# One fused recurrent block on one core: new due times for the planned order, the experts' first block among them

## The reference

```python
xn = layernorm(x)
x  = x + attention16heads(xn) * silu(moe(xn))            # 160 experts, top 8, plus a shared one
xn = layernorm(x)
x  = x + mamba2layers(xn) * silu(coupling_net_3cycles(xn))

def moe(x):
    probs = sigmoid(x @ router_w.T + bias)
    w, idx = top_k(probs, 8); w = 2.5 * w / (sum(w) + 1e-9)
    return sum_k w_k * (silu(x @ gate[idx_k].T) @ down[idx_k].T) + shared(x)

def mamba(x, p):                       # state of 16, 256 inner channels, scan along the sequence
    u = silu(conv4(x @ in_w)); delta = softplus(...)
    h[t] = exp(delta * A) * h[t-1] + delta * B[t] * u[t];  y[t] = C[t] . h[t]
    return (y + D * u) * silu(z) @ out_w
```

## Time and profile before

| | before |
|---|---|
| median of 3 runs | 2323.13 us (2319.16 to 2328.2) |
| profiled execution | 2325.84 us, span 2324.0 us, mean granted clock 0.887 |
| PE busy | 1946.7 us (84%) |
| DVE busy | 1648.5 us (71%) |
| POOL busy | 1500.2 us (65%) |
| ACT busy | 1312.4 us (56%) |
| DMA | 321.50 MB, mean 138 GB/s |

### The profile page before, as it was taken

One profiled execution on the slowest core, in us unless ns is written; L12 is line 12 of the kernel. 1 busy time (PEld: TensorE's weight loads), 2 busy tenths in 40 slices (PEclk: granted clock), 3 DMA queues, 4 the chain that ended last, 5 costly groups with the idle time before them and its releaser, 6 DMA issues. The chain is left out here.

```text
span 2324.0 us, 29708 instructions
## 1 busy us (share of the span) xinstructions
PE 1946.7 (84%) x8440; PEld 878.5 (38%) x8440; DVE 1648.5 (71%) x3485; ACT 1312.4 (56%) x2685; POOL 1500.2 (65%) x1476
## 2 busy tenths in 40 slices
PE   4576499999998898986787787899898898899976
PEld 2343266665655555553333332222222222222221
DVE  3877165665656756667466414999999899999998
ACT  3354154554534445354577656777766666667663
POOL 0388485774355745407653002999999999999997
PEclk9779799999999999998788888898888898888896
DMA  9931387786665756641110004555555555555552
GB/s 379 395 86 59 89 243 216 227 237 190 202 191 150 221 147 174 188 120 51 42 35 24 1 3 106 116 120 115 114 114 119 124 125 129 130 129 128 129 125 43
DMA packets 210968, 321.50 MB, mean 138 GB/s; under 512 B 28914, under 2 KB 102644, under 8 KB 210420
## 3 DMA queue, kind: packets, MB, share of 16 engines
q1 hardware_dynamic: 194420, 286.02, 45.2%
q0 software_dynamic: 16384, 33.59, 5.1%
HBM read 207.29 MB, written 112.20 MB: 137 GB/s over the span
## 5 line engine op out<-in xcount | busy, mean ns | idle before, releaser
L1498 DVE TENSOR_TENSOR_SCAN db<-pa,db 128x512 f32<-128x512 f32 x512 | 597.5, 1209 | 46.1 <-POOL db L1549 29.7
L1549 POOL TENSOR_TENSOR db<-dur,bb 128x1024 f32<-128x1024 f32 x256 | 596.9, 2356 | 48.5 <-DMA bb<-bc_scratch 39.7
L1479 ACT ACTIVATE pa<-dlr,an 128x510 f32<-128x510 f32 x512 | 340.2, 681 | 188.2 <-DVE db L1498 187.3
L1022 POOL DMA_INDIRECT yg<-y_disp,idx x256 | 257.6, 1006 | 185.6 <-DMA y_disp<-yb 85.7
L725 POOL DMA_INDIRECT x_disp<-xt,idx x256 | 254.4, 994 | 149.2 <-DVE p L699 93.4
L860 ACT ACTIVATE pr<-sm,nbi 128x128 f32<-128x128 f32 (+1 forms) x512 | 228.1, 447 | 209.4 <-DVE nbi L883 204.6
L907 POOL TENSOR_SCALAR pr<-pr,rcp 128x128 f32<-128x128 f32 x320 | 134.9, 432 | 244.7 <-DVE rcp L892 242.3
L1404 PE MATMUL pb<-db,rw_all 128*32 128x512 f32 x1024 | 209.9, 698 | 79.3 <-DVE db L1504 47.8
L883 DVE CUSTOM_DVE_ANT_0 sm<-pa,rw_front 128x128 f32<-128x128 f32 (+1 forms) x512 | 161.1, 352 | 105.2 <-PE pa L780 104.7
L143 ACT ACT_TABLE_LOAD x146 | 187.3, 1283 | 56.3 <-DVE lg L587 16.3
L790 PE MATMUL pb<-rw_all,pr 128*128 128x128 f32 x768 | 143.3, 298 | 73.7 <-DVE ptt L877 49.6
(11 more groups left out here) (292 smaller groups left out, 3387.7 us busy)
## 6 DMA issues: line engine op xcount, KB each, us to landing
wb<-in_wexp SPq DMA_DIRECT2D x576, 96.0 KB
x_disp<-yb SPq DMA_DIRECT2D x8, 4608.0 KB, 30.1
xb<-x_disp SPq DMA_DIRECT2D x144, 256.0 KB
y_disp<-yb SPq DMA_DIRECT2D x144, 256.0 KB
dlr<-d_scratch SPq DMA_DIRECT2D x128, 256.0 KB, 5.3
dur<-d_scratch SPq DMA_DIRECT2D x128, 256.0 KB, 8.3
bb<-bc_scratch SPq DMA_DIRECT2D x64, 256.0 KB
d_scratch<-dl SPq DMA_DIRECT2D x32, 256.0 KB, 5.8
```

What stands on the lines that cost most here:

```text
L1022: e.e.indirect_dma_start(out=YG[:, t % 2, j, :], out_offset=None, in_=YD[h], in_offset=bass.IndirectOffsetOnAxis(ap=IDX[:, c:c + 1], axis= ...
L1479: e.e.activation(decay(a).rearrange("p (b l) -> p b l", b=2)[:, :, 1:256], DLR[:, h % 2, i % 4, :].rearrange("p (b l) -> p b l", b=2)[:, : ...
L1498: e.e.tensor_tensor_scan(hk(a), decay(a), hk(a), 0.0, ALU.mult, ALU.add).then_inc(s_scan, 1)
L1549: e.e.tensor_tensor(DB[:, b % ND, :, :], DUR[:, h % 2, 2 * (b % 2):2 * (b % 2) + 2, :], BB[:, b // 2 % 4, :].rearrange("p (o l) -> p o l", ...
```

## The change

Only numbers of `PL` change: no instruction is added or taken away, no tile, no semaphore. So every engine has the same instructions in another order. The quads' first due time goes from 1.3234 to 1.4811 and their step from 2.6979 / 72 to 2.605 / 72; some sixty other offsets move a little.

```diff
--- before.py
+++ after.py
@@ -41,87 +41,87 @@
 
 
 PL = {'net_a': 0.3,
- 'quad0': 1.3234,
- 'quads': [2.6979, 2.6979],
+ 'quad0': 1.4811,
+ 'quads': [2.605, 2.605],
  'after0': 22,
  'after': 14,
  'back': [7.0971, 7.4103, 7.7, 8.32],
- 'pick0': 3.5729,
- 'picks': 3.5546,
+ 'pick0': 3.5611,
+ 'picks': 3.532,
  'pick1': 6.8429,
  'picks1': 0.2953,
  'net': [7.2386, 8.4094],
  'nets': [0.06, 0.0472],
  'qload': 1.9826,
- 'qcopy': 0.31,
- 'qgate': 0.8265,
- 'qtanh': 1.2037,
- 'qstt': 1.2651,
- 'qdown': 1.7277,
- 'qyb': 2.0102,
+ 'qcopy': 0.3818,
+ 'qgate': 0.7876,
+ 'qtanh': 1.1564,
+ 'qstt': 1.301,
+ 'qdown': 1.708,
+ 'qyb': 2.0168,
  'qout': 2.8324,
  'sum': 10.1825,
- 'b_sg': 0.2077,
+ 'b_sg': 0.1951,
  'b_sth': 0.3731,
- 'b_hs': 0.4677,
- 'b_cb': 0.5793,
+ 'b_hs': 0.4663,
+ 'b_cb': 0.4909,
  'b_th': 0.5906,
  'b_gs': 0.7618,
- 'b_m': 0.7165,
+ 'b_m': 0.7504,
  'b_c': 0.9108,
- 'b_sq': 0.7871,
- 'b_v': 0.7661,
- 'b_ln': 0.91,
+ 'b_sq': 0.833,
+ 'b_v': 0.8202,
+ 'b_ln': 0.9574,
  'b_x': 0.5141,
  'u_ex': 0.8912,
- 'u_pt': -0.8853,
+ 'u_pt': -0.8732,
  'u_sm': 0.4089,
  'u_pn': 0.2408,
- 'u_k': -2.1136,
- 'u_kc': -1.6411,
- 'norm0': 0.0219,
- 'norm': 0.0142,
+ 'u_k': -2.2911,
+ 'u_kc': -1.621,
+ 'norm0': 0.0238,
+ 'norm': 0.0111,
  'normu': 0.0118,
  'routeA': [0.0993, 0.0297],
- 'routeB': [0.547, 0.0536],
- 'placeA': [0.35, 0.016],
- 'placeB': [0.9637, 0.0164],
+ 'routeB': [0.5312, 0.0536],
+ 'placeA': [0.361, 0.016],
+ 'placeB': [0.9872, 0.0151],
  'unit0': 0.4143,
  'PG': [0, 1, 1, 1, 1, 1, 0, 0],
- 'sends': 73,
- 'l_m': 0.0097,
+ 'sends': 74,
+ 'l_m': 0.0136,
  'l_xi': [0.1133, 0.1982],
- 'l_z': [0.1831, 0.2458],
- 'l_bc': 0.349,
+ 'l_z': [0.1831, 0.2705],
+ 'l_bc': 0.3492,
  'l_dt': [0.3955, 0.3884],
  'l_ds': [0.6084, 0.716],
  'l_out': 0.4456,
  'l_c': -2.4568,
  'l_y': [4.4386, 6.8066],
- 'l_sq': -0.0665,
- 'l_ln': 0.0497,
- 'l_u': [0.1938, 0.3298],
- 'l_bf': 0.411,
- 'l_ab': [0.4595, 0.4956],
+ 'l_sq': -0.0481,
+ 'l_ln': 0.0464,
+ 'l_u': [0.187, 0.3298],
+ 'l_bf': 0.379,
+ 'l_ab': [0.4595, 0.4733],
  'l_ex': 0.5125,
- 'l_w': 0.5414,
- 'l_v': 0.49,
- 'l_lp': 0.5743,
- 'l_dl': [0.6663, 0.7761],
- 'l_da': -2.8788,
+ 'l_w': 0.5459,
+ 'l_v': 0.5264,
+ 'l_lp': 0.5653,
+ 'l_dl': [0.6663, 0.7804],
+ 'l_da': -2.8649,
  'l_hn': 0.0022,
- 'l_du': [0.7876, 0.8567],
+ 'l_du': [0.8161, 0.8567],
  'l_dr': -4.8619,
- 'l_pc': 1.5235,
- 'l_fin': 0.6595,
- 'l_bo': 0.3062,
- 'l_bi': -14.8957,
+ 'l_pc': 1.5337,
+ 'l_fin': 0.6725,
+ 'l_bo': 0.3135,
+ 'l_bi': -14.9793,
  'l_bi0': 0.4477,
  'l_ci': -11.1275,
  'l_do': [0.7083, 0.8679],
  'l_uo': [0.5681, 0.6088],
- 'l_di': [0.7229, 1.0777],
- 'l_ui': [0.7033, 1.0502],
+ 'l_di': [0.7203, 1.0751],
+ 'l_ui': [0.7012, 1.0502],
  'layers': 8.6489}
```

## The result

The change makes the kernel slower by 0.9%: 2338.95 us (median of 6 runs, 2337.75 to 2352.91) beside 2321.14 us (6 runs, 2315.13 to 2328.2), ratio 1.009, 95% interval 1.0071 to 1.0109. The forecast, 2334 us, is 5 us off. The profiled execution took 2352.91 us, 14 us above its median, so places are compared with it, and sizes with the medians.

What follows compares the result with a forecast made beforehand. PE's list was taken to bound the attention with quads, nearly full POOL the scans. Terms -22 - 2 + 0 + 34 = +10 on the profiled 2325.8 gave 2335.8, or 2334 us for the median, range 2300 to 2346.

Steps and rivals of the forecast that it cites:

- The first block: Group 0, before the first quad: 21.8 us of PE work moves into its 29.49 us wait; taken as -22 us.
- The norms: Ahead of the routing: norms written more nearly in one piece, first scatters earlier; -2 us, between -6 and +3.
- Denser quads: Attention groups: 3.6% more quads per group, the last ending sooner; taken as 0, bounds +6 and -4 us.
- The prediction's own sign: Start of the scans: one not some 24 us before 1440 us would sink the front's term.
- The layers: `l_du`: Fifteen scan stages: `du` half 0 falls behind drive 13, 2.3 us later each; +34 us, bounds 0 and +36.
- The layers: `l_fin`: Scan stages with the group's last products: they come one drive later, still before `du`; cost 0.
- the prediction's natural trial: Six stages with last products (2.5 us) before `du`: interval 56.5 against 54.4 us, read as `du`'s delay costing 2.1.
- A: Scan stages: the delay of `du` is absorbed, only the front's gain is left; 2299 us, chance 0.16.
- B: Front: the block's shift gives nothing back, the layers' +34 stands alone; 2357 us, chance 0.10.
- C: Front and layers both as forecast: 2334 us, between 2324 and 2345; chance 0.72.

Runs made afterwards that it cites:

- e3: The kernel before with only quad0 = 1.4811 and quads = 2.605 (first block and quads' density) changed: 2315.0 us, ratio 0.9958.
- e5: The kernel after with all layers' offsets (`l_`) set back, so only front and middle changed: 2306.22 us, 0.992 of the kernel before.
- e4: The kernel before with only the norms' offsets changed (norm0 0.0238, norm 0.0111): 2321.01 us, ratio 0.999.
- e1: The kernel after with `l_du[0]` put back to 0.7876, all else as changed: 2322.31 us, 0.9983 of the kernel before.
- e8: The kernel before with each load of `bb` and C split into four transfers, 32 rows outermost: 2311.55 us, ratio 0.9952.
- e9: The kernel after with each load of `bb` and C split into four transfers, on another chip: 2499.51 us, 0.9962 of the kernel before there.
- e10: The changed front with the layers' offsets of before and the `bb` and C loads split, on another chip: 2506.65 us, 0.9996 of the kernel before.
- e6: The kernel before with only `l_fin` changed, from 0.6595 to 0.6725: 2333.59 us, ratio 1.0044.
- e11: The kernel before with `du` half 0 one drive earlier (`l_du[0]` = 0.73), on another chip: 2501.8 us, ratio 0.9972.

## Why the prediction was right

**The first block** (-22). The mechanism and its place hold: L809 ahead of the first quad, group 1's projection at 371.35 us where "about 371" was forecast, and a wait of 7.93 us in e3 where 7.6 was worked out from the rows. In the full change it is 13.21: the attention ends sooner there, as with e4's norms, and the rows land at 262.12, no earlier than before.

**The norms** (-2). e4 can't tell it from nothing, and its interval holds it. The first quad came 3.1 us sooner there, but not in the full change (262.12 beside 261.44).

**Denser quads** (0, from +6 to -4). Here the front came out short. At group 1 it was 26 us ahead (369.21 in e5 against 394.81), and 17 us came through; e3, block and density alone, kept 10.8 of the forecast 22, outside its interval, and lost 12 in group 5. The sum reckoned with PE's work per group only; in group 5 PE also stands longer for DVE. Whether the density or the block's shift does that is not shown. The whole front is worth -17, beside -24, a difference that e5's interval (-25 to -12) doesn't exclude. The prediction's own sign, scans that start some 24 us sooner, was seen in e1 and e5 (first b = 8 24 and 25 us ahead of the kernel before); in the profile of the kernel after, itself 14 us above its median, it is 13.

**The layers: `l_du`** (+34). Right in place and in size: +34.5 alone. The forecast intervals were 56.4 and 58.5; after has 56.3 and 59.2. That the transfers absorb next to nothing of the 2.3 us was the author's estimate: the share of 0.26 over the last ten microseconds is a mean, and no run shows which engines finish last. What the runs show is that 1.8 to 2.2 us of it came through in each plain stage, and from the other side, in e8, e9 and e10: with each load of `bb` and C as four transfers (a share of 1.00 near the end, in e8) the plain intervals are 54.5 and 54.6 with the layers' offsets of before and 53.5 with the changed ones.

**The layers: `l_fin`** ("still before `du`: 0"). Wrong by itself: +10 alone (e6). The step looked at POOL's list and not at SP's, where the output store waits for the last product and the `dl` store of half 0 waits behind it. The kernel before shows it already, in the stage of POOL's row at 1741.74:

```profile
1744.40 0.36 SPq L1634 DMA_DIRECT2D out<-x  x1
...
1745.44 0.50 SPq L1607 DMA_DIRECT2D d_scratch<-dl  x1
1750.26 0.32 SPq L1611 DMA_DIRECT2D d_scratch<-du  x1
1751.10 1.77 SPq L1621 DMA_DIRECT2D dlr<-d_scratch  x4
```

The loads begin 5.7 us behind the `dl` store, as in e1 and e6, and half a microsecond behind the end of the `du` store's issue: the two ways are level there, and either alone delays the loads. So the prediction's natural trial (2.5 us ahead of `du` cost 2.1) measured this way as much as `du`'s. In the sum it hardly showed, since it delays loads that `du` delays too: all the layers' offsets together cost 33 to 35, not 45. That the layers' sum of +34 came out although `l_fin` isn't free is luck. The forecast was +10.9 on its median of 2323.13 and the measured change is +17.8; the front's -17 in place of -24 accounts for the 7 us between.

**The rivals.** A (absorbed, 2299) fell with the intervals at 56.3. B (the front gives nothing back, 2357) fell with e5. C stands, with -17 for the front and +35 for the layers, against the forecast -24 and +34.

## What to carry to other kernels

Where a stage's transfers are released by a chain through one issuing queue, an edit of a few hundredths of an offset can be paid in every stage (0.0285 in `l_du` cost 34.5 us here, and 0.013 in `l_fin`, paid in six stages, 10); look for each item in the queue that waits for the moved instruction, and for everything queued behind it, before costing a move at nothing. Two delays of the same chain didn't add up (34.5 and 10 us alone, 33 to 35 together with the rest), so undoing one of them gave back less than it cost alone. And the form of some loads can be the reason that the order on another engine matters at all: with each load of `bb` and C as four transfers, the offsets that had cost 33 us cost nothing (53.5 us a plain stage with them, 54.5 and 54.6 without).

## What had not been expected

- The four `dur` issues of half 1 take 7.62 us in the stage shown of the kernel before, 6.63 us in that of the kernel after, and 1.85 us in e8, where the loads are split; those of half 0 take 1.85 us in each of the three. What holds the issues up is not shown.
- On two chips every kernel took some 185 to 195 us more; in e11 PE stood 65.2 us of it at a single line of the routing for no event that the profile shows. A gain that lies in filling one wait of the front was not seen there.
- With the same code ahead of them, but for e4's norms, the scans began between 1446.6 and 1460.5 us in five profiled executions. Differences under some 10 us at one place are read from several kernels or from the medians.
